# A two-stage attention block on one core: rings of exponentials and of pieces from two places to three, landing buffers from three to two, and new orders of the steps on every engine

## The reference

```
h  = group_norm(x) * gn_w + gn_b                 # 32 groups
q, k, v = wq h + bq, wk h + bk, wv h + bv
x1 = x + wo (v softmax_rows(q^T k / 16)^T) + bo                 # block 0
att = x1 x1^T ; att_c = softmax(max(att) - att)                 # 256 x 256
fb, fc, fd = wb x1 + bb, wc x1 + bc, wd x1 + bd                 # 32, 32, 256 rows
pos = fd softmax_rows(fb^T fc)^T                                # block 2
out = (beta att_c x1 + x1) + (alpha pos + x1)
```

## Time and profile before

| what | us |
|---|---|
| median of three runs | 431.94 (431.71 to 432.14) |
| profiled execution, its own time | 434.71 |
| its span, first to last instruction | 432.8 |
| PE matmul busy | 414.9 (96%) |
| PE weight loads busy | 282.2 (65%) |
| DVE busy | 308.0 (71%) |
| ACT busy | 242.5 (56%) |
| POOL busy | 53.8 (12%) |

### The profile page before, as it was taken

How to read it: one execution, slowest core, us unless ns; L and a number is a source line. 1 busy time by engine, 2 the same in 40 slices (tenths; PEclk the granted TensorE clock), 3 DMA queues, 4 the chain that set the end, 5 groups by cost and what they waited for, 6 DMA issues and landing times.

```text
span 432.8 us, 5686 instructions
## 1 busy us (share of the span) xinstructions
PE 414.9 (96%) x2090; PEld 282.2 (65%) x2090; DVE 308.0 (71%) x476; ACT 242.5 (56%) x324; POOL 53.8 (12%) x51
## 2 busy tenths in 40 slices
PE   1999999999999999999999999999998999999994
PEld 1788856676778565767867656667764665676552
DVE  3487878578889689875867887664485989888511
ACT  1567663556774656674547765634555777856300
POOL 1400053010000810010100521020010200000000
PEclk9989999999999999999999999999999999999998
DMA  8445469360063597552592468650058764567741
GB/s 236 133 160 91 92 87 218 72 123 2 0 123 73 105 237 145 102 96 48 122 220 48 78 119 177 115 97 2 0 142 151 145 120 78 97 145 130 163 98 48
DMA packets 140395, 48.02 MB, mean 111 GB/s; under 512 B 135824, under 2 KB 137296, under 8 KB 140368
## 3 DMA queue, kind: packets, MB, share of 16 engines
...
## 4 chain that ended last, share of the span: by engine, by line
PE 87%; DMA 4%; DVE 3%; ACT 3%; issue 2%; SPq 0%; POOLq 0%; POOL 0%; ACTq 0%; DVEq 0%
PE sum_ps L814 13%; PE sum_ps L815 13%; PE sum_ps L816 13%; PE score_ps L814 13%; PE score_ps L816 12%; PE score_ps L815 12%; PE score_ps L968 3%; PE score_ps L939 3%; DMA x<-in_x_dram 2%; DMA x<-in_L_conv_wo_dram 2%; PE score_ps L949 2%; ACT exps L432 1%; PE score_ps L824 1%; DVE g_l L540 1%; PE score_ps L976 1%
## 5 line engine op out<-in xcount | busy, mean ns | idle before, releaser
L432 ACT ACTIVATE exps<-score_ps,negmax 128x1024 f32<-128x1024 f32 x64 | 71.2, 1113 | 73.6 <-DVE negmax L673 56.8
L689 DVE SCALAR_TENSOR_TENSOR pieces<-exps,recip,pieces 128x1024 f16<-128x1024 f32 x64 | 87.0, 1366 | 19.6 <-ACT pieces L442 19.4
L673 DVE TENSOR_REDUCE negmax<-score_ps 128x1 f32<-128x1024 f32 x64 | 77.6, 1217 | 16.5 <-PE score_ps L816 13.0
L442 ACT ACTIVATE pieces<-exps,recip 128x1024 f16<-128x1024 f32 x64 | 72.4, 1142 | 20.0 <-DMA land<-pieces 11.3
L814 PE MATMUL score_ps<-xn_h,g_h 128*128 128x512 f32 x128 | 53.4, 417 | 1.1 <-DVE fd_l L712 0.7
L815 PE MATMUL score_ps<-xn_l,g_h 128*128 128x512 f32 x128 | 50.7, 396 | 0.0
L816 PE MATMUL score_ps<-xn_h,g_l 128*128 128x512 f32 x128 | 50.6, 396 | 0.0
L814 PE MATMUL sum_ps<-land,fd_h 128*128 128x512 f16 x128 | 48.8, 381 | 0.0
L814 PE MATMUL sum_ps<-land,v_h 128*128 128x512 f16 x128 | 48.8, 381 | 0.0
L815 PE MATMUL sum_ps<-land,fd_h 128*128 128x512 f16 x128 | 48.5, 379 | 0.0
L816 PE MATMUL sum_ps<-land,fd_l 128*128 128x512 f16 x128 | 48.5, 379 | 0.0
...
## 6 DMA issues: line engine op xcount, KB each, us to landing
...
land<-pieces SPq DMA_TRANSPOSE x64, 4.4
...
```

The lines of the kernel that those rows point to most:

```text
L432: act.activation(exps[:, n % 2, :], score_ps[s][:, :], ACT.Exp, bias=negmax[:, n % RING:n % RING + 1], scale=1.0, accum_out=rowsum[:, n % ...
L442: act.activation(pieces[:, n % 2, 0, :], exps[:, n % 2, :], ACT.Copy, scale=recip[:, n % RING:n % RING + 1]).then_inc(high_piece, 1)
L673: dve.tensor_reduce(negmax[:, n % RING:n % RING + 1], score_ps[s][:, :], AX.X, ALU.max, negate=True)\
L689: dve.scalar_tensor_tensor(pieces[:, n % 2, 1, :], exps[:, n % 2, :], recip[:, n % RING:n % RING + 1], pieces[:, n % 2, 0, :], ALU.mult, A ...
```

## The change

`HALVES` goes from 3 to 2, and a new `AHEAD` = 3 takes the place of the 2 in the rings `exps` and `pieces`: `exp` of tile n now waits for `b` of tile n - 3, and `a` of tile n for the landing of tile n - 3. The four lists are new ones. The number and kinds of the steps are the same, but for their order.

```diff
-HALVES = 3
+HALVES = 2
+AHEAD = 3
...
-        exps = sb("exps", [P, 2, N])
-        pieces = sb("pieces", [P, 2, 2, N], f16)
+        exps = sb("exps", [P, AHEAD, N])
+        pieces = sb("pieces", [P, AHEAD, 2, N], f16)
         land = sb("land", [P, HALVES, 2, NT, QC], f16)
...
             def exponential(use):
-                if n >= 2:
+                if n >= AHEAD:
-                    act.wait_ge(both_pieces, n - 1)
+                    act.wait_ge(both_pieces, n - AHEAD + 1)
...
             def piece(use):
-                if n >= 2:
+                if n >= AHEAD:
-                    k, j = turn_of(TILES[n - 2])
+                    k, j = turn_of(TILES[n - AHEAD])
...
 PE_ORDER = """
...
-    V.2.0 S0.2.5 O2.0.1x1 V.2.1 FD.1.0 O0.2.0x3 AT.1 S2.1.2 S2.1.3 O0.2.0x5 VAR.3 S2.1.4 FD.1.1 S0.2.6 ET.1
...
+    O2.0.1x1 S2.1.2 O2.0.1x1 AT.1 O2.0.1x1 V.2.1 MX.1 S0.2.4 O0.2.0x1 ET.1 S0.2.5 O0.2.0x7 S2.1.3 FD.1.0 S0.2.6
```

More of the change, by code:

```diff
@@ L33 @@
[L33 to L36, removed]
+    G.0.0 BG W S0.0.0 S0.0.1 S0.0.2 S0.0.3 V.0.0 SV G.0.1 V.0.1 S0.0.4 S0.0.5 MEAN.1 S0.0.6 VAR.1 S0.0.7
+    O0.0.0x6 G.1.0 O0.0.0x2 S0.1.0 S0.1.1 S0.1.2 O0.0.1x1 MEAN.2 S0.1.3 O0.0.1x7 FBC.0.0 V.1.0 V.1.1 MX.0 G.1.1
@@ L43 @@
[L43 to L52, removed]
@@ L53 @@
-    exp2.2.4 a2.2.3 exp2.2.5 a2.2.4 x1h.3.1 hFD.2.1 a2.2.5 exp2.2.6 exp2.2.7 hXT.3.1 hFBC.3.0 a2.2.6 a2.2.7
-    hFBC.3.1 base.3.0 cA.3 base.3.1 exp2.3.0 exp2.3.1 a2.3.0 expE.3 a2.3.1 exp2.3.2 hFD.3.0 a2.3.2 exp2.3.3
-    hET.3 a2.3.3 exp2.3.4 exp2.3.5 a2.3.4 exp2.3.6 a2.3.5 hFD.3.1 a2.3.6 exp2.3.7 a2.3.7
+    ldx1.1 hG.0.0 hW xb.0.0 xb.0.1 xb.1.0 xb.1.1 exp0.0.0 exp0.0.1 exp0.0.2 a0.0.0 a0.0.1 a0.0.2 exp0.0.3 hV.0.0
+    hG.0.1 hV.0.1 a0.0.3 exp0.0.4 exp0.0.5 a0.0.4 a0.0.5 exp0.0.6 xnh.1.0 xnh.1.1 exp0.0.7 a0.0.6 a0.0.7 hG.1.0
@@ new lines @@
+    x1h.0.0 exp0.1.0 exp0.1.1 a0.1.0 a0.1.1 exp0.1.2 a0.1.2 exp0.1.3 a0.1.3 hFBC.0.0 x1h.0.1 hV.1.0 hV.1.1
+    hG.1.1 hFBC.0.1 hXT.0.0 exp2.0.0 exp2.0.1 hFD.0.0 a2.0.0 hXT.0.1 a2.0.1 base.0.0 base.0.1 exp2.0.2 exp2.0.3
+    cA.0 a2.0.2 a2.0.3 exp0.1.4 expE.0 exp0.1.5 hFD.0.1 hET.0 a0.1.4 a0.1.5 exp0.1.6 xnh.2.0 xnh.2.1 exp0.1.7
+    x1h.1.0 exp2.0.4 a0.1.6 a0.1.7 a2.0.4 exp2.0.5 hG.2.0 hXT.1.0 a2.0.5 exp2.0.6 exp0.2.0 a2.0.6 exp2.0.7
+    a0.2.0 a2.0.7 hFBC.1.0 exp0.2.1 a0.2.1 x1h.1.1 exp0.2.2 a0.2.2 exp0.2.3 a0.2.3 hG.2.1 hXT.1.1 hFBC.1.1
@@ new lines @@
+    base.1.0 base.1.1 hV.2.0 exp2.1.0 a2.1.0 cA.1 exp2.1.1 exp2.1.2 expE.1 hV.2.1 a2.1.1 ldx1.2 hET.1 exp0.2.4
+    xb.2.0 a2.1.2 xb.2.1 exp0.2.5 a0.2.4 a0.2.5 exp2.1.3 hFD.1.0 a2.1.3 exp0.2.6 hFD.1.1 a0.2.6 x1h.2.0 hXT.2.0
+    xnh.3.0 xnh.3.1 exp0.2.7 a0.2.7 exp2.1.4 exp2.1.5 exp2.1.6 a2.1.4 a2.1.5 a2.1.6 hG.3.0 exp2.1.7 a2.1.7
+    exp0.3.0 a0.3.0 hFBC.2.0 hXT.2.1 exp0.3.1 exp0.3.2 a0.3.1 exp0.3.3 x1h.2.1 a0.3.2 hG.3.1 a0.3.3 base.2.0
+    base.2.1 hV.3.0 exp0.3.4 hFBC.2.1 a0.3.4 cA.2 exp0.3.5 a0.3.5 exp0.3.6 a0.3.6 hV.3.1 expE.2 exp0.3.7 ldx1.3
@@ L56 @@
+    a0.3.7 exp2.2.0 a2.2.0 exp2.2.1 exp2.2.2 hET.2 xb.3.0 xb.3.1 exp2.2.3 a2.2.1 a2.2.2 hFD.2.0 exp2.2.4 x1h.3.0
+    exp2.2.5 a2.2.3 a2.2.4 exp2.2.6 hXT.3.0 a2.2.5 x1h.3.1 hFD.2.1 a2.2.6 hXT.3.1 base.3.0 exp2.2.7 hFBC.3.0
+    a2.2.7 base.3.1 hFBC.3.1 cA.3 exp2.3.0 exp2.3.1 a2.3.0 expE.3 a2.3.1 exp2.3.2 a2.3.2 exp2.3.3 exp2.3.4
+    a2.3.3 a2.3.4 exp2.3.5 hET.3 exp2.3.6 hFD.3.0 a2.3.5 a2.3.6 hFD.3.1 exp2.3.7 a2.3.7
 """.split()
 DVE_ORDER = """
-    lG.0.0 lW bn.1 max0.0.0 max0.0.1 lS r0.0.0 max0.0.2 r0.0.1 b0.0.0 max0.0.3 b0.0.1 r0.0.2 lG.0.1 r0.0.3
@@ L60 @@
[L60 to L64, removed]
@@ new lines @@
+    r0.2.2 max0.2.3 b0.2.2 r0.2.3 b0.2.3 lG.2.1 lXT.1.1 lFBC.1.1 lV.2.0 max2.1.0 gvar.3 r2.1.0 xn.3.0 xn.3.1
+    sA.1 max2.1.1 max2.1.2 aA.1 minE.1 fo.0.1.1 fo.0.1.0 b2.1.0 r2.1.1 sF.1 lV.2.1 nE.1 max0.2.4 b2.1.1 lET.1
+    r2.1.2 max0.2.5 r0.2.4 b2.1.2 r0.2.5 b0.2.4 b0.2.5 fx.2.0.0 max2.1.3 fx.2.0.1 r2.1.3 lFD.1.0 b2.1.3 max0.2.6
+    r0.2.6 lFD.1.1 b0.2.6 lXT.2.0 max0.2.7 r0.2.7 b0.2.7 max2.1.4 max2.1.5 max2.1.6 r2.1.4 r2.1.5 r2.1.6
+    fo.1.0.1 fo.1.0.0 b2.1.4 b2.1.5 b2.1.6 lG.3.0 max2.1.7 r2.1.7 max0.3.0 b2.1.7 r0.3.0 b0.3.0 fx.2.1.0
@@ L306, in _ @@
                     land[:, k % HALVES, :, :, cols(j)].rearrange("p a t q -> p (a t) q"),
-                    pieces[:, n % 2, :, :].rearrange("p a n -> p (a n)")).then_inc(landed[k % HALVES][j], 16)
+                    pieces[:, n % AHEAD, :, :].rearrange("p a n -> p (a n)")).then_inc(landed[k % HALVES][j], 16)
             for s in range(2):
```

70 lines of the change are left out of this document (35 added, 35 removed).

## The result

The changed kernel took **441.05 us** in the median (437.29 to 442.63, 4 runs), the kernel before 432.04 (431.71 to 433.13, 4 runs): a ratio of 1.0172, 95% interval [1.0119, 1.0225]. The forecast was 430.5 with a range to 433.0. The sign was wrong and the time lies 8 us outside.

A forecast was written before the change was run, and what follows sets the result against it. PE was taken as the bound, with only its gaps (4 us) to change. Terms -2.0 - 0.9 + 0.5 + 0.3 + 0.3 + 0.4 = -1.4 us off the median 431.94 gave 430.5 us, range 429.0 to 433.0.

The forecast's parts named there:

- part 1: Load of x for image 3, after sum `O2.1.1`: data in time with 1.6 us slack, both PE gaps go, gain 2.0 us.
- part 6: Two landing buffers: transposes wait for the sum two before, but the third place of `pieces` bears this; cost 0.
- Where PE is full, and that only gaps count: PE busy all 92.3 us from 238.5 to 330.8; only gaps between its starts, 4 us in all, can change the time.
- Part 2: Load of x for image 2, after `O2.0.1`: ACT still waits some 4 us, but its customers come later; gain 0.9 us.
- Part 3: `FD.0.0` to `S2.0.2` share a PSUM place; read-out takes 2.7 us against 2.3 of PE work; loss 0.5 us.
- Part 4: First scores: late read-out delays the exponential for `S0.0.6`, `VAR.1` no longer waits; loss 0.3 us (-0.3 to 0.9).
- Part 5: `O2.2.0` to `O2.2.1` with nothing between: PE stands 0.5 us for DVE's read-out, before 0.25; loss 0.3 us.
- the places with little slack: Places with slack under 0.5 us (`ET.1`, `S2.3.0`, `FBC.2.1`): loss 0.4 us together.
- a load is late again: Held transposes beside stores and load after `O2.1.1` make it 2 us later: 432.5 us; chance 0.24 shared with another rival.
- The slower rival: PE waits for a landing at `O2.1.0`, third step, by 1.1 to 3.4 us: 433.5 us (432.8 to 434.5); chance 0.13.
- Its gaps should be in all of them, so I take the sum off the median: Gaps read in the profiled execution of 434.71 us taken as present in all; sum subtracted from the median of 431.94.
- a gap after the bias of image 3: Sign that the forecast is wrong: a gap after the bias steps on the loaded image 3.

The follow-up runs named there:

- e1: The changed kernel run again with no edit: 434.49 us in the median (432.87 to 446.0, 10 runs); its profiled execution took 433.83.
- e12: The changed kernel run a fourth time with no edit, on another chip: 440.09 us in the median (435.38 to 441.76, 4 runs).
- e2: The kernel before, its four lists kept, with the new rings (HALVES 2, AHEAD 3): 445.54 us, 1.0286 of before.
- e11: The kernel before with the first 512 columns of image 3 loaded earlier, nothing else changed: 432.42 us, 0.9961 of before.
- e3: The changed kernel with three landing buffers instead of two, room made by reusing other buffers: 433.11 us, 0.9988 of before.
- the first trace: Profile of the changed kernel's first measurement, no further edit: the profiled execution took 437.29 us, span 435.4.
- e5: The changed kernel run a third time with no edit, on another chip: 439.56 us in the median (434.29 to 443.15, 10 runs).

## Why the prediction was wrong, point by point

What failed are the landing of the load in part 1 and the 0 of part 6. For all parts but the first, e1 is the trace to read, an execution in which the load is not very late. Its first scores begin at 23.90 (before: 23.93) and its `O2.3.1` at 413.01 (before: 413.88). So between these two traces the change gains **0.9 us** where the load isn't late; the sum had said 1.4. The shortest executions don't bear out even that much: on the three chips 432.87, 434.29 and 435.38 us for the changed kernel, 431.35, 431.75 and 430.58 for the one before.

- **Where PE is full, and that only gaps count**: right. From 238.5 to 330.8 us the changed kernel's PE is busy for 91.83 us at a clock of 1.00, before 92.30. In the long executions one thing comes on top: behind the gap the starts themselves lie 0.43 us apart.
- **Part 1, the load for image 3 (-2.0)**: this step failed. Its timetable put the issue 5.4 us after the end of `O2.1.1`, bound by ACT's exponential. The last matmul of that sum starts at 319.06 in e12; VectorE reads it out from 319.55 to 321, as assumed; GpSimd issues the two stores from 320.60 on, taking 1.30 us; they land after 4.3; the load goes off at 325.88, about 6.6 after the end, bound by the stores. Then the text took 8.4 "as before" for the load. That figure was itself the second transfer beside a transpose: in the trace of before the two transfers landed after 3.7 and 8.0 us, the transpose issued between them after 9.3. In e12 the second landed after 13.0 and the first use is at 339.27, 13.4 after the issue; PE stood 3.73 us and lost 2.9 more in clock. The slack was 1.6 us and the lateness 6. In e1 it is less: one gap of 0.47 us idle is left before the transposes at 329.2, where before had two. I put that at 0.6 us lost and 1.4 gained.
- **Part 2, the load for image 2 (-0.9)**: right. ACT still waits for it (2.64 us at 222.02), and no PE gap follows.
- **Part 3 (+0.5)**: right, 0.52 us of idle time at 116.7 for `fd_l` in e1.
- **Part 4, the first scores (+0.3)**: too small. `S0.1.0` starts at 71.91 in e1 and at 70.99 before, 0.9 later, at the bound that part 4 had named. Its working was right in that `S0.0.6` waits for an exponential (0.45 us) and that `VAR.1` no longer waits; not foreseen was a wait for GpSimd's low part of x at `G.1.0`, which no row of before shows. e1's rows:

```profile
51.99 0.47 PE L815 MATMUL score_ps<-xn_h,g_h 128*128 128x512 f32 x1 [0.45 <-ACT exps L433]
66.03 0.50 PE L815 MATMUL score_ps<-xn_h,a_w_h 128*128 128x512 f32 x1 [0.30 <-POOL xn_l L351]
```

- **Part 5 (+0.3)**: right in kind, 0.3 short. The rows below show 0.89 us from start to start in place of 0.22, so 0.7 lost. The 0.25 that the text gave to before was mostly a misreading: 0.71 us from 377.40 to 378.11, where two 32-bit matmuls behind a 16-bit one take 0.65 elsewhere too (257.65 to 258.30), so the loss is some 0.6. The five parts as measured add up to -0.3, the marks to -0.9; the places with little slack, put at +0.4, seem to have cost nothing.

```profile
376.15 0.38 PE L817 MATMUL sum_ps<-land,fd_l 128*128 128x512 f16 x1
377.04 0.48 PE L815 MATMUL sum_ps<-x_h,et_h 128*128 128x512 f32 x1 [0.51 <-DVE x L780]
```

- **Part 6, two landing buffers (0)**: wrong, and it is the change's real price. The text said "I take 0, as no load falls beside it", having looked for it at the sums up to `O2.1.0`. There nothing happened. At `O2.1.1` a load does fall beside it, and the text knew: it is the rival "a load is late again".
- **That rival** had the mechanism word for word, held transposes that start just before the stores and the load, and gave it 432.5 us. It was **mis-sized** (2 us of lateness, where e12 had 6), by three assumptions: that part 1 can fall only to 0, though the exponentials behind a late load can stop PE for longer than before; that a wait costs only its own length, though in the long executions one of 3.7 us cost 2.9 more in clock; and that the landing is one number, though the second transfer of the same load took 5.6 us in e1 and 13.0 in e12.
- **The slower rival** had the right chain at a place where it did not occur: no sum of e1 or e12 waited for a landing. With the old order (e2) it decides the time.
- **The executions' own spread** was taken from three runs that agreed within 0.1%. On the other chips the same kernel came between 430.6 and 437.3, so a difference of under 1 us can't be told from these medians, and the marks inside the traces had to decide it.
- **"Its gaps should be in all of them, so I take the sum off the median"**: not shown, and the runs speak against it. The gaps were read in an execution of 434.71 us and taken off a median of 431.94. e11, whose trace has none of the three large gaps, took 431.57 at its shortest, and e3 432.78, while before came down to 430.58 and 431.35 on their chips. The short executions of before may never have had the late load; none of them has a trace.

What the prediction said would show it wrong, "a gap after the bias of image 3", is what the first trace, e5 and e12 showed.
